# Where the transposes of the probabilities stand in a head pair of a two-layer cross attention, and where their copies stand between the exponentials

## The reference

```python
# layer 0: 32 query heads of 16, 8 key/value heads, additive mask
q, k, v = x @ Wq + bq, ctx @ Wk + bk, ctx @ Wv + bv
attn = softmax(q @ k.T / 4 + mask0)            # per head, 100 x 361
x = layernorm((attn @ v) @ Wo + bo + x) * gamma + beta
# layer 1: 16 heads of 32, boolean mask, context normalised first
a = layernorm(ctx) * ln_gamma + ln_beta
q, k, v = x @ Wq.T, a @ Wk.T, a @ Wv.T
attn = softmax(where(mask1, q @ k.T / sqrt(32), -inf))
out = x + tanh(gate) * ((attn @ v) @ Wo.T)
```

## Time and profile before

| what | value |
|---|---|
| median of 3 runs | 1230.87 us (1230.49 to 1233.23) |
| the profiled execution | 1232.87 us, its span 1231.1 us |
| PE busy | 1151.5 us, 94% of the span |
| weight loads (PEld) | 942.6 us, 77% |
| DVE busy | 806.0 us, 65% |
| ACT busy | 749.8 us, 61% |
| POOL busy | 251.5 us, 20% |
| granted TensorE clock, mean | 0.99 of full speed |
| share of PE in the chain that ended last | 72% (issue 13%, ACT 6%, DVE 4%) |

### The profile page before, as it was taken

How to read it: one execution, slowest core, us unless ns; L and a number is a source line. 1 busy time by engine, 2 the same in 40 slices (tenths; PEclk the granted TensorE clock), 3 DMA queues, 4 the chain that set the end, 5 groups by cost and what they waited for, 6 DMA issues and landing times.

```text
span 1231.1 us, 32229 instructions
## 1 busy us (share of the span) xinstructions
PE 1151.5 (94%) x10003; PEld 942.6 (77%) x10003; DVE 806.0 (65%) x2386; ACT 749.8 (61%) x2163; POOL 251.5 (20%) x264
## 2 busy tenths in 40 slices
PE   4989999999999999999999999999999999999997
PEld 4678778786877778787777878778787877878786
DVE  4365666767576776757677675766767586676735
ACT  3374656747475674747567474765747476574744
POOL 1041212111131211113121121312122131211210
PEclk9699999999999999999999999999999999999999
DMA  7665536547363654726365472735647273564500
GB/s 237 163 181 112 155 74 151 133 97 189 72 161 85 139 143 88 196 67 167 86 132 151 88 194 59 174 89 121 156 93 184 63 171 84 125 166 92 142 8 8
DMA packets 77821, 153.77 MB, mean 125 GB/s; under 512 B 10384, under 2 KB 47056, under 8 KB 77152
## 3 DMA queue, kind: packets, MB, share of 16 engines
q1 hardware_dynamic: 77792, 153.40, 51.3%
HBM read 113.72 MB, written 39.65 MB: 125 GB/s over the span
## 4 chain that ended last, share of the span: by engine, by line
PE 72%; issue 13%; ACT 6%; DVE 4%; DMA 1%; POOL 1%; DVEq 1%; ACTq 1%; SPq 0%; POOLq 0%
PE PJ L363 16%; PE TP L414 13%; PE OA L434 5%; PE SCO L400 5%; PE SCO L680 5%; PE SCO L458 4%; PE PJ L466 4%; ACT PR L1050 4%; PE PJ L376 4%; PE SCO L404 4%; PE OA L439 3%; PE SCO L363 2%; DVE SCO L824 2%; ACT PT L1061 1%; PE SCO L665 1%
## 5 line engine op out<-in xcount | busy, mean ns | idle before, releaser
L1050 ACT ACTIVATE PR<-SCO,MN 100x361 f32<-100x361 f32 x768 | 426.5, 567 | 144.8 <-DVE MN L824 143.2
L824 DVE CUSTOM_DVE_ANT_0 SCO<-SCO,MK 100x361 f32<-100x361 f32 x768 | 399.7, 551 | 126.0 <-PE SCO L400 99.7
L414 PEld LDWEIGHTS TP<-ident,PR 100*128 100x128 f32 x2304 | 222.5, 141 | 79.4 <-ACT PT L1061 28.5
L414 PE MATMUL TP<-ident,PR 100*128 100x100 f32 x2304 | 270.0, 253 | 6.7 <-ACT PT L1061 4.4
L1061 ACT ACTIVATE PT<-TP 121x600 f32<-121x600 f32 x256 | 172.2, 672 | 57.1 <-PE TP L414 55.1
L400 PE MATMUL SCO<-K0S,Q0S 128*100 128x362 f32 x512 | 165.8, 374 | 37.4 <-ACT PR L1050 36.1
L1050 ACT ACTIVATION_READ_ACCUMULATOR PR<-SCO,MN 100x1 f32 x768 | 159.7, 208 | 0.0
L834 DVE COPY PT<-TP 121x600 f32<-121x600 f32 x128 | 100.2, 783 | 65.6 <-PE TP L414 62.0
L400 PEld LDWEIGHTS SCO<-K0S,Q0S 128*100 128x100 f32 x512 | 74.8, 167 | 62.3 <-ACT PR L1050 60.0
L824 DVE DVE_READ_ACCUMULATOR2_ANT MN<- 100x1 f32 x768 | 108.5, 141 | 0.0
L1215 POOL TENSOR_TENSOR K1F<-K1F,KB 128x364 f32<-128x364 f32 x64 | 50.8, 794 | 259.8 <-DVE K1F L816 259.8
(11 more groups left out here) (140 smaller groups left out, 1814.8 us busy)
## 6 DMA issues: line engine op xcount, KB each, us to landing
K1S<-k_scr SPq DMA_DIRECT2D x128, 364.0 KB, 6.1
k_scr<-K1HL SPq DMA_DIRECT2D x64, 364.0 KB, 3.2
Q0S<-q_scr SPq DMA_DIRECT2D x128, 100.0 KB, 4.0
K0S<-k_scr SPq DMA_DIRECT2D x64, 182.0 KB, 5.0
AT<-ctx_cols SPq DMA_DIRECT2D x16, 722.0 KB, 9.4
V<-ctx_rows SPq DMA_DIRECT2D x16, 484.0 KB
q_scr<-QHL SPq DMA_DIRECT2D x16, 400.0 KB, 2.5
k_scr<-K1HL SPq DMA_DIRECT2D x32, 182.0 KB, 3.0
```

The lines of the kernel that those rows point to most:

```text
L414: last = pe.transpose(TP[:, k % 2, c * T:(c + 1) * T], PR[0:T, k % NPR, c * SP:c * SP + P], ident[0:T, 0:T])
L824: dve.tensor_tensor_reduce(out=bank, in0=bank, in1=mask[0:T, :], scale=scale, scalar=3.4e38, op0=ALU.add, op1=ALU.min, accum_out=MN[0:T, k ...
L1050: act.activation(PR[0:T, k % NPR, 0:S], SCO[0:T, k % 3, 0:S], ACT.Exp, bias=MN[0:T, k:k + 1], scale=-1.0, accum_out=SM[0:T, k:k + 1]).then ...
```

## The change

No instruction is added or taken away. Three things move.

- **PE, layer 0**: the six transposes of pair p-2 go from behind the filling of pair p to directly behind its two scores.
- **PE, layer 1**: the filling goes from between the two scores to behind the transposes. The order in a pair is thus first score, second score, transposes, filling, in both layers.
- **DVE and ACT**: a copy out of `TP` now stands between the pair's first and second head (between the two shifts, or between the two exponentials). In DVE's list, it is also two pairs' distance rather than three behind its own scores. `keys1_scaled` moves behind both shifts of its pair, and ACT's `keys1_high(b, 3)` goes from step 4 to step 5.

```diff
@@ PE, layer 0 @@
                         score(b, k)
+                    if p >= 2:
+                        transpose_probs(b, p - 2)
+                    elif not first:
+                        transpose_probs(b - 1, NPAIR - 2 + p)
                     if p in PV1_TAIL and not first:
...
                         out1(b - 1, range(*OUT1_STEPS[p]))
-                    if p >= 2:
-                        transpose_probs(b, p - 2)
-                    elif not first:
-                        transpose_probs(b - 1, NPAIR - 2 + p)
@@ DVE, layer 0 @@
-                    if p % 4 == 0 and (p > 0 or not first):
-                        if p > 0:
-                            probs_out(b, p - 3)
-                        else:
-                            probs_out(b - 1, NPAIR - 3)
-                    elif p == 2 and not first:
-                        probs_out(b - 1, NPAIR - 1)
                     if first and p in (4, 6, 8, 10):
                         keys1_scaled(b, p // 2 - 2)
-                    elif not first and p == 0:
+                    shift(b, 2 * p)
+                    if p == 1 and not first:
+                        probs_out(b - 1, NPAIR - 1)
+                    elif p % 4 == 3:
+                        probs_out(b, p - 2)
+                    shift(b, 2 * p + 1)
+                    if not first and p == 0:
                         keys1_scaled(b, 2)
                     elif not first and p == 3:
                         keys1_scaled(b, 3)
-                    for k in (2 * p, 2 * p + 1):
-                        shift(b, k)
@@ DVE, layer 1 @@
-                    if p in (20, 22):
-                        probs_out(b, p - 3)
                     shift(b, 2 * p)
+                    if p in (19, 21, 23):
+                        probs_out(b, p - 2)
+                    shift(b, 2 * p + 1)
                     if more and p == 17:
                         keys1_scaled(b + 1, 0)
                     elif more and p == 20:
                         keys1_scaled(b + 1, 1)
-                    shift(b, 2 * p + 1)
@@ ACT, layer 0 @@
                         exps(b, 2 * p - 2)
+                        if p >= 3 and (p - 3) % 4 != 1:
+                            probs_out(b, p - 3)
+                        elif p == 1 and not first:
+                            probs_out(b - 1, NPAIR - 2)
                         exps(b, 2 * p - 1)
...
-                    if p >= 3 and (p - 3) % 4 != 1:
-                        probs_out(b, p - 3)
-                    elif p == 1 and not first:
-                        probs_out(b - 1, NPAIR - 2)
...
-                    elif not first and p == 4:
+                    elif not first and p == 5:
                         keys1_high(b, 3, first)
```

More of the change, by code:

```diff
@@ L715, in batch @@
                     score(b, 2 * p)
+                    if p > 16:
+                        pe.wait_ge(prob, NH * b + 2 * p - 1)
+                    if p == 16:
+                        pe.wait_ge(rep_dve, 2 * b + 1)
+                    elif p == 17:
+                        pe.wait_ge(rep_dve, 2 * b + 2)
+                    score(b, 2 * p + 1)
+                    if p >= 18:
+                        transpose_probs(b, p - 2)
                     if more and p in K1_EARLY:
@@ L726, in batch @@
                         repeated_keys(3)
[L727 to L733, removed]
                     if p == 23:
@@ L746, in batch @@
                         last.then_inc(gb_mm, 1)
-                    if p >= 18:
-                        transpose_probs(b, p - 2)
             batch(0, True, True)
@@ L954, in batch @@
                         ctx_mean(b + 1)
-                probs_out(b, 13)
                 if more:
@@ L1018, in _ @@
             batch(NB - 1, False, False)
-            probs_out(NB - 1, NPAIR - 3)
             repeat_sums(NB - 1, 2)
```

## The result

| kernel | median, us | ratio to before, 95% interval |
|---|---|---|
| before | 1231.84 | |
| changed | 1283.51 (1282.8 to 1284.27) | 1.0422 (1.0406 to 1.0437) |

The change makes the kernel 4.2% slower. The profiled span grew from 1231.1 to 1282.0 us. I cut both PE timelines into three stages a batch: layer 0 (first score of pair 0 to the first query matmul behind pair 15), the middle part (from there to the matmuls that repeat the queries of layer 1, line 696), and layer 1 (from there to the next batch's first score).

What follows compares the result with a forecast made beforehand. PE's own work sets layer 1, and waits add a few us in layer 0. Losses of 34.5 + 1.7 + 6.6 + 0 = 42.8 us on 1232.87 give 1275.7; less 2.0 for the median, 1274 us, range 1244 to 1297.

Steps and rivals of the forecast that it cites:

- Rules A and B: S = a pair's first score: next pair's second score from S+2.01 us (A), its transposes from S+2.56 where ACT copies (B).
- Layer 1: 2.3 forecast: Layer 1, batches 0 to 14: both rules and late keys lose 2.3 us a batch, 34.5 us in all.
- The side road of the keys: Layer 1: `keys1_scaled` starts later, so ACT's `keys1_high` waits for POOL, delaying exponential 36, copy 16 and pair 19's transposes.
- a hole of about 1.3 us: Layer 1, sign of the late keys: PE has a gap of about 1.3 us between pair 19's scores.
- Layer 0: +0.45 forecast: Layer 0: wins 0.8 in the first three pairs, loses it to rule B; +0.45 us a batch, 6.6 in all.
- The middle part: 0 forecast: Between the layers: exponential 31 comes later, but pair 15's transposes stand two query fillings later and find it done; 0.
- The last batch: Layer 1 of the last batch: rules A and B in turn over five pairs, +1.7 us.
- Faster: Layer 0's score waits go, rule B doesn't bind, layer 1 loses rule A's 0.8 alone; 1189 us, chance 0.06.
- no change: Whole kernel: layer 0 gains what layer 1 loses by rule A; 1231 us, chance 0.04.
- slower but little: The keys' side road in layer 1 is hidden and layer 0 gains its lower bound; 1249 us, chance 0.10.
- Slower still by waits: Waits cost 3.0 us a batch in layer 1 and 1.3 in layer 0; 1297 us, above that chance 0.04.
- The clock's fall: Attention stages: PE's clock falls to 1.2 GHz; 1390 us or so if halved in one tenth of busy time, chance 0.02.

Runs made afterwards that it cites:

- l1_spread: keys_between with the first two filling matmuls of layer 1 between the two scores, the rest behind the transposes; 1265.52 us, ratio 1.028 to the kernel before.
- keys_between: Changed kernel with only `keys1_scaled` of blocks 0 and 1 back between the shifts of pairs 17 and 20; 1273.23 us, ratio 1.0341 to the kernel before.
- l1_alone: Kernel before with the change in layer 1 alone (PE and DVE); 1262.11 us, ratio 1.0249.
- l0_act_alone: Kernel before with one edit: in layer 0 ACT's copies stand between the two exponentials; 1240.37 us, ratio 1.0078.
- l1_undone: Changed kernel with layer 1 as before, layer 0 keeping the change; 1245.06 us, ratio 1.0121 to the kernel before.
- short_copies_l1: Changed kernel with ACT's layer 1 copies moving 8 of 300 columns a head, not in the first batch; 1265.88 us, ratio 1.0287 to the kernel before.
- short_copies_l0: Changed kernel with ACT's layer 0 copies moving 8 of 300 columns a head, from the second batch on; 1252.15 us, ratio 1.0185 to the kernel before.
- l1_pe_undone: Changed kernel with PE's list of layer 1 as before and DVE's as changed; 1280.20 us, ratio 1.0401 to the kernel before.

## Why the prediction was right, and where it wasn't

**Direction and mechanism** were right, and the time of 1283.5 lies in the range, 9.5 us over the forecast of 1274. That it is so near is partly luck. The profiled execution is 8.1 over the 1275.7 of the sum, and the 8.1 are in the main +7.5 in layer 1 of the first fifteen batches and +5.5 in layer 0 of the last fifteen, against -3.8 in the middle part and -1.8 in layer 0 of the first batch, where the forecast had 0. The rest of the 9.5 is the 2.0 taken off for the median, which lies only 0.3 under the profiled execution after the change.

**Rules A and B** held in the places named. The first scores of pairs 18, 20, 21 and 22 were worked out for 28.57, 33.11, 34.75 and 37.06 (us behind 600, in the old trace's time), and came at 28.58, 33.27, 34.96 and 37.29 when the new trace is laid on the old at line 696 (22.01 us later). Taking the copy's cost away gave back the 1.1 us, net of pair 22. What I had wrong about rule B is its independence: l1_spread shows that it takes over the delay of DVE's copy.

**Layer 1: 2.3 forecast, 2.9 measured.** The term that was mis-sized is PE's own time in a pair. I took 0.46 + 0.83 from transposes to the next first score. Behind transposes, the second matmul of filling comes 0.25 and not 0.17 after the first, and a set of transposes that waited itself takes 0.51 to the next instruction: 655.61 to 656.97 is 1.36, 657.88 to 659.30 is 1.42. Some 0.1 in each of five pairs, and the 0.2 that PE takes from `out_half` to the next score (664.44, released by nothing that the profile shows), make the 0.6.

**The side road of the keys** was worked out for 0.7 us a batch and gave 0.73 (keys_between). The second score and the transposes of pair 19 came within 0.05 us of their places. The sign given for it, "a hole of about 1.3 us", was too long: the scores start 1.06 apart, and PE is idle for 0.73. And layer 1, said to grow from 14 us to over 16, grew from 15.4 to 18.3; 14 is near PE's busy time there.

**Layer 0: +0.45 forecast, +0.78 measured**, with the pairs' starts within 0.4 us of those worked out (pair 3 5.5 for 5.3, pair 6 12.5 for 12.6, pair 12 27.1 for 27.0, end 36.2 for 35.9). The sign came out and the size within the bounds, by two terms that I had told in one: the gain in the first pairs belongs to the edit of layer 1 (l1_alone: -0.89), the loss to the edit of layer 0. The reason that I gave for a gain, "an exponential is no longer held by a copy in front of it", doesn't stand alone (l0_act_alone: +0.6, and the scores of layer 0 wait as long as before, 3.5 us).

**The middle part: 0 forecast, -0.2 a batch measured**, -3.8 in all. The step "the transposes of pair 15 stand two fillings of queries later and still find it done" was right as to the loss and looked for no gain. With the transposes of pair 13 ahead of pair 15's filling, the copy that frees those of pair 14 is no longer waited for: they start 0.86 us behind the first query matmul (701.52 - 700.66) in place of 1.03 (676.03 - 675.00).

**The last batch**: +1.7 forecast, +1.5 measured from line 696 on.

**The rivals.** Faster and no change fall with the eleven waits for ACT's copy, and slower but little falls with keys_between. Slower still by waits, with layer 1 at its upper bound of 3.0 a batch, was nearly met there (2.9), but layer 0 stayed at 0.8. The clock's fall came true in one small place, below.

## What to carry to other kernels

Two consumers of one chain shouldn't stand together in an in-order list where the chain is longer than a turn: filling between them covers the way round (in layer 0, 34.2 us a batch in place of 36.0 with nothing else moved). Work behind which a wait is hidden can't be moved without asking what it hid, and a helper's copy placed between two heads holds the second head whenever what it copies comes late. An edit of several engines' lists is one edit: in layer 0, single parts of this one gave +3.6, +0.6 and -0.9 us a batch, where the whole gave +0.8.

## What the runs showed of the hardware that I had not expected

In the first batch of the changed kernel the granted clock fell to 1.2 GHz for some 3 us, behind PE's waits of 1.58 and 0.24 us at 57.7 and 58.3 us. The windows (us; busy us per engine; clock):

```profile
56.00:60.00 4.00, 2.17 (x13) 1.85 (x13) 2.85 (x9) 3.02 (x6) 0.00 (x0) 0.92 0.54 188
60.00:61.00 1.00, 1.00 (x4) 0.61 (x3) 0.80 (x3) 1.00 (x4) 0.28 (x1) 0.50 0.90 359
...
63.00:64.00 1.00, 1.00 (x8) 1.00 (x7) 0.00 (x0) 1.00 (x3) 1.00 (x1) 1.00 0.90 211
```

Before, with waits of 1.6, 1.2 and 1.8 us in the same 18 us, the clock stayed at 1.00. So my reading of that row as proof against a fall was too strong. The row also began late: from 50 to 52 us the same trace has a granted clock of 0.50. By the Trainium skill, "TensorE: Matmul & The Clock Gate", section "Part 1: The HAM clock gate", idle time lowers the clock and sustained work brings it back; this trace agrees for that one place in the order of events, while the kernel before, with more waiting there, shows no fall. The two windows of a later batch, shown with the result, have 1.00.

Layer 0 of the first batch took from 47.5 to 52.3 us in these kernels, in no order that their edits explain. Seven of them have the same layer 0 in the first batch, and there the granted clock goes along with it in part: a mean of 0.93 with 47.5 us (l1_undone, short_copies_l1, short_copies_l0), 0.90 with 49.1 and 49.2 (l1_pe_undone, the changed kernel), 0.87 with 52.3 (keys_between), but 0.83 with 50.8 (l1_spread). So single times can differ by some us for this reason alone, and the -1.8 of the first batch is no effect of the change that could be told from it.
